# A graph network of two layers on one core: the numbers for VectorE's node one-hots are read from PSUM

## What is computed

```python
e = leaky_relu(xl[src] + xr[dst], 0.2)                 # layers 0 and 1
logits = einsum('ehc,hc->eh', e, att)
m = segment_max(logits, dst); ex = exp(logits - m[dst])
denom = segment_sum(ex, dst)
out = segment_sum(xl[src] * (ex / denom[dst])[..., None], dst) + b
# layer 2: e = leaky_relu(s1[:, src] + s2[:, dst]), Wh = h @ W in place of xl
```

## Time and profile before

| | |
|---|---|
| median of 3 runs | 4124.04 us |
| profiled execution | 4115.89 us, span 4114.1 us |
| granted TensorE clock, mean | 0.947 |
| PE, PEld busy | 3659.4 us (89%), 2722.7 us (66%) |
| DVE busy | 3149.5 us (77%) |
| POOL busy | 2804.3 us (68%) |
| ACT busy | 1229.2 us (30%) |
| POOL's 2496 gathers L692 | 2610.5 us busy, 800.1 us idle before them |
| edge stages of layers 0, 1, 2, by the first and last gather | 188 to 1311, 1549 to 2674, 2866 to 3993 us |

### The profile page before, as it was taken

The page is one execution under the profiler, slowest core; times in us unless marked ns, Lnnn a source line. Parts: engine busy times, 40 slices in busy tenths (PEclk is TensorE's granted clock), DMA queues, the critical chain, the costliest instruction groups (busy, mean ns, idle before and its releaser), DMA issues. The chain is left out here.

```text
span 4114.1 us, 121899 instructions
## 1 busy us (share of the span) xinstructions
PE 3659.4 (89%) x31817; PEld 2722.7 (66%) x31818; DVE 3149.5 (77%) x8748; ACT 1229.2 (30%) x4200; POOL 2804.3 (68%) x2941
## 2 busy tenths in 40 slices
PE   6699999999999898999999999977788777877875
PEld 5577777777776676777777777745455554555543
DVE  6667877787788665787787787875688788888886
ACT  4433333333333563333333333324111111111113
POOL 5577777777775127777777777723777777777760
PEclk9899999999999999999999999999788889888889
DMA  4354444444443225444444444435545545554544
GB/s 101 107 141 127 132 131 133 127 132 132 132 127 96 62 67 135 131 132 132 127 132 132 131 126 132 126 107 176 136 136 139 137 132 139 139 135 133 139 107 125
DMA packets 333899, 521.05 MB, mean 127 GB/s; under 512 B 152887, under 2 KB 219617, under 8 KB 333809
## 3 DMA queue, kind: packets, MB, share of 16 engines
q0 software_dynamic: 120320, 338.39, 30.1%
q1 hardware_dynamic: 213489, 181.58, 15.4%
HBM read 484.14 MB, written 35.46 MB: 126 GB/s over the span
## 5 line engine op out<-in xcount | busy, mean ns | idle before, releaser
L692 POOL DMA_INDIRECT gathered<-table,idx x2496 | 2610.5, 1046 | 800.1 <-issue 545.9
L1131 PE MATMUL pS<-gathered,Dm 128*128 128x264 f32 x4992 | 1706.2, 425 | 90.6 <-DVE Dm L1537 49.4
L1525 DVE TENSOR_TENSOR acc_mem<-acc_mem,pS 128x264 f32 x2496 | 1041.4, 417 | 133.0 <-PE pS L1131 108.7
L1068 PE MATMUL pZ<-DT,x 128*128 128x128 bf16 x9984 | 1083.7, 221 | 11.8 <-DVE DT L1488 9.0
L1068 PEld LDWEIGHTS pZ<-DT,x 128*128 x9984 | 867.9, 99 | 339.4 <-issue 61.6
L853 ACT ACTIVATE reluT<-pZ 128x256 f32<-128x256 f32 x1664 | 636.9, 383 | 1301.8 <-PE pZ L1074 1182.5
L1074 PE MATMUL pZ<-ident,gathered 128*128 128x128 f32 x3328 | 937.5, 282 | 15.9 <-DMA gathered<-table,idx 15.7
L1131 PEld LDWEIGHTS pS<-gathered,Dm 128*128 128x128 f32 x4992 | 793.0, 200 | 234.1 <-DVE gathered L1554 112.6
L1554 DVE TENSOR_TENSOR gathered<-gathered 128x512 f32<-128x512 f32 x1248 | 852.4, 683 | 65.0 <-ACT gathered L870 64.1
L1537 DVE TENSOR_TENSOR Dm<-iota_row,rel_items 128x256 f32<-128x256 f32 x1248 | 516.5, 414 | 0.0
L1074 PEld LDWEIGHTS pZ<-ident,gathered 128*128 128x128 f32 x3328 | 470.7, 141 | 20.3 <-DMA gathered<-table,idx 18.9
(11 more groups left out here) (230 smaller groups left out, 3372.3 us busy)
## 6 DMA issues: line engine op xcount, KB each, us to landing
DT<-rel_dram SPq DMA_DIRECT2D x156, 512.0 KB
gathered<-table,idx POOLq DMA_INDIRECT x2496
flags<-flag_dram SPq DMA_DIRECT2D x1664, 8.0 KB
span_row<-flag_dram SPq DMA_DIRECT2D x1664, 0.1 KB
table<-xls SPq DMA_DIRECT2D x147, 132.0 KB, 1.9
flags<-flag_dram SPq DMA_DIRECT2D x416, 32.0 KB
gathered<-table SPq DMA_DIRECT2D x98, 132.0 KB, 2.1
gathered<-in_x SPq DMA_DIRECT2D x98, 128.0 KB, 2.1
```

Source lines behind the costliest of these rows:

```text
L692: nc.gpsimd.indirect_dma_start(out=G[:, b, i, :], out_offset=None, in_=tab[l], in_offset=bass.IndirectOffsetOnAxis(ap=idx[:, b, i:i + 1], ...
L1068: mm = nc.tensor.matmul(z_slot(i)[:, half], x3[:, bass.ds(tk[i], 1), s, half].rearrange("p o c -> p (o c)"), moving, start=(s == 0), stop= ...
L1131: nc.tensor.matmul(pS[:, i % 4, 0:ROW], Dm[:, i % 8, :], G[:, at[0], at[1], :], start=True, stop=True).then_inc(seg_done, 1)
L1525: link(v.tensor_tensor(acc_at(n), acc_at(n), pS[:, n % 4, 0:ROW], ALU.add))
```

## The change

The numbers 0 to 127 are copied once, before the first group of layer 0, into columns 288 to 415 of each of the four banks of `pS`. From then on a one-hot that follows an `add` reads its numbers there, in the bank whose sums have just been added, and no longer from `iota_row` in SBUF. One-hots without an add before them (in the first groups of a layer) still use `iota_row`. `rel` stays in SBUF and stays the second operand.

```diff
                 if l == 0:
                     clear_sums()
+                    dve.wait_ge(xr_ready, TILES)
+                    dve.wait_ge(xls_ready, TILES)
+                    pre(v.tensor_copy(pS[:, :, IOTA:IOTA + P], iota_row[:].unsqueeze(1).to_broadcast([P, 4, P])))
...
                             rel = rel_items[:, bass.ds(k0 + (2 * s + 2 - 3 * GI // 2), 2)]
-                            ins = v.tensor_tensor(Dm[:, 2 * p % 8:2 * p % 8 + 2, :], iota_row[:].unsqueeze(1).to_broadcast([P, 2, P]),
+                            numbers = pS[:, 2 * s % 4, IOTA:IOTA + P] if adds else iota_row[:]
+                            ins = v.tensor_tensor(Dm[:, 2 * p % 8:2 * p % 8 + 2, :], numbers.unsqueeze(1).to_broadcast([P, 2, P]),
                                                   rel.unsqueeze(2).to_broadcast([P, 2, P]), ALU.is_equal)
                             if adds:
                                 ins.then_inc(added, 1)
...
 EARLY = 4
+IOTA = 288
```

## The result

| | before | after |
|---|---|---|
| median of 19 runs each, us | 4125.71 (4120.17 to 4129.43) | 4119.15 (4106.96 to 4123.68) |
| ratio, 95% interval | | 0.9983 (0.9976 to 0.9990) |
| profiled execution (span) | 4115.89 (4114.1) | 4120.86 (4119.0) |
| first to last gather, layers 0, 1, 2 | 1122.7, 1125.4, 1127.6 | 1122.7, 1122.4, 1129.7 |

The change is worth 6.6 us by the medians, 0.17%, where 19 were forecast. The two profiled executions alone stand the other way round: that of the kernel before, 4115.89, is shorter than all 19 runs beside it.

The account below looks back on a forecast made before the run. It took layer 2 to be bound by POOL's 832 gathers and layers 0 and 1 by PE's pace. Terms -18 - 1 + 0 = -19 us, from 4124.04, gave 4105; own range 4096 to 4117, overall range 4085 to 4127.

Parts of the forecast that it names:

- The price of the one-hot: DVE's one-hots reading PSUM: 414 ns as before, so no cost; bounds 10 ns less or more, 12 us of DVE.
- Something of DVE's holds a gather, and PSUM as one input ends it: All layers: two-SBUF DVE instructions stall POOL's gathers at their start; under one-hots 20.3, 20.1 and 15.7 us, ended by PSUM.
- Nothing is freed: Rival, chance 0.18: the one-hot's second input, still in SBUF, keeps all 408 gather stalls; 4124 us, within 5.
- The copies: Start of kernel: one tensor_copy of 512 elements on DVE, covered by a 13.99 us wait; costs nothing, 0.7 us without cover.
- Layers 0 and 1: Gain for both layers together from one-hots no longer holding gathers: 1 us, bounds 0 and 6.
- PE's own pace sets the end: Layers 0 and 1: PE, at 21.62 us per 16 items, and not POOL sets when the layer ends.
- the gain is given back at once: Layers 0 and 1: a gather freed of 0.14 us lets the next start earlier under the same L1554, ending no sooner.
- All of it comes off: Rival, chance 0.10: layers 0 and 1 are bound by POOL too, so all 56 us go; 4068 us.
- 18, with 8 as the low bound: Layer 2, bound by POOL's gathers: 18 us shorter without one-hot stalls, low bound 8 (half given back), high 25.
- the re-timing: Layer 2: unheld gathers start the next ones earlier; a gather-by-gather walk made the 15.7 us gain 18 to 22.
- within 0.2%: Whole kernel: outcome "same", a difference of at most about 8.2 us; chance 0.24, against faster 0.66 and slower 0.10.
- slower: Rival, chance 0.10: in layers 0 and 1 freed gathers are caught by L1554 instead, 0.53 us more per group; 4161 us.

Follow-up runs that it names:

- h6_swap: The changed kernel with the one-hots' two inputs exchanged, rel in SBUF first and the numbers in PSUM second; 4118.39 us against 4122.88, ratio 0.9986.
- q4_sbuf_weigh_l2: As p3_weigh_l2, but all one-hots read their numbers from SBUF again; 4065.76 us against 4124.64 for the kernel before, ratio 0.9861.
- q5_weigh_l01: The changed kernel with the weighting factors of layers 0 and 1 read from PSUM, softmax weighting left out there; 4112.57 us against 4124.64, ratio 0.9970.
- p3_weigh_l2: The changed kernel with layer 2's weighting factors read from PSUM, softmax weighting left out there; 4057.51 us against 4121.77 for the kernel before, ratio 0.984.
- e3_weigh_l2: Same kernel as p3_weigh_l2, run when the kernel before itself took 5244 to 5323 us; ratio 0.9995 (0.9969 to 1.0020).

## Why the prediction was right or wrong

**The price of the one-hot: right.** 414 ns forecast, 414 measured, with 1239 of them reading PSUM; in h6_swap they take 400 to 422. By the figures of the Trainium skill, "VectorE: DVE Perf Modes", section on the TRN2 errata, it would be some 65 ns dearer, an estimate; this case's rows don't show that: L1541 has one PSUM operand and the same 414 as the earlier trace rows with none.

**Something of DVE's holds a gather, and PSUM as one input ends it: right.** The 408 stalls under one-hots, 56 us over the three layers, are gone, in either order of the operands. *Nothing is freed* is out. One thing the prediction read too narrowly: not all 408 gathers began under their one-hot. In the kernel before 19 of them, 16 in layer 2, began up to 0.07 us ahead of it, and lost 6.5 us together:

```profile
2937.29 1.29 POOL L692 DMA_INDIRECT gathered<-table,idx  x1 [0.30 <-issue]
...
2937.35 0.41 DVE L1537 TENSOR_TENSOR Dm<-iota_row,rel_items 128x256 f32<-128x256 f32 x1
```

The Trainium skill, "SBUF — State Buffer", section "Who interferes with whom", says that two SBUF inputs contend with GpSimd instructions that read SBUF and one doesn't; the tensor_tensor rows of this case agree, with 0.95 us against 1.09 and 1.31 for a gather. Its other remark, that tensor_tensor left DMAs alone in a probe, doesn't hold for the gathers here: 1.09 against 0.95 us, in the rows of q4_sbuf_weigh_l2 and h6_swap.

**The copies: right.** DVE waits for 13.65 us behind them. DVE's timeline in the changed kernel, which answers to the earlier trace rows:

```profile
201.84 0.69 DVE L1496 COPY pS<-iota_row 128x512 f32<-128x512 f32 x1
...
217.02 0.43 DVE L1571 TENSOR_TENSOR_SCAN F<-flags,cT 128x128 f32<-128x128 f32 x1 [13.65 <-ACT cT L849]
```

**Layers 0 and 1: right in time, wrong in mechanism.** The forecast was 1 us, bounds 0 and 6; by the profiled executions layer 0 has 0.0 and layer 1 3.0 (in h6_swap -0.9 and 4.1). "PE's own pace sets the end" stood the test of q5. But "the gain is given back at once", under the next L1554, was wrong. What was named as its sign, L692's mean within 3 us of now and more stall under L1554, failed: the means fell from 1045 to 1005 and 1003 ns, and the stall under the weighting fell too, from about 50 us to 37.7 and 36.0. POOL now runs ahead until it meets the limit of the 32 slots, and waits there. Timeline of layer 0:

```profile
726.86 0.94 POOL L692 DMA_INDIRECT gathered<-table,idx  x1 [1.17 <-POOLq L358]
```

Such waits of over 0.02 us beyond the usual 0.30 number 41 in layer 0 and 44 in layer 1, where there had been 0 and 6. Most of these gathers begin 0.81 us after the L1068 that frees a slot. The waits hold 33.7 us in layer 0, which is what the gathers lost in length. The mistake was to follow POOL with DVE's times as they were in the earlier trace rows and with no limit on how far POOL may be ahead. A walk that keeps one side fixed can't show where the other comes to rest. *All of it comes off* is out with it.

**Layer 2: the step that failed.** "18, with 8 as the low bound" was put on layer 2's stretch; the gain came out at -2.1 in the changed kernel, and at 3.1 and 2.5 in h6_swap and q5_weigh_l01, whose layer 2 does the same (all against the one trace of the kernel before). The mean gather of the layer, which was to fall by 20 to 25 ns, went from 1048 to 1052. Who bounds the layer was right (p3_weigh_l2), that the 15.7 us leave the one-hots was right, and they are worth some time where no weighting can take them over (q4 against p3). The term that was mis-sized is the re-timing. It was worked out as a gain of 2 to 6 us on top of 15.7 ("18 to 22"), and was a loss of 12.6 to 17.8: 15.7 less the 3.1, 2.5 or -2.1 that arrived. The weighting took the stalls over: 64.4 us under it where there were 53.9. The re-timing rests on one assumption, "DVE's instructions stay at their distance from the landing that opens their group". I ran the same walk, with no stalls under one-hots, on the changed kernel's own distances: it gives 1127.2, where the trace has 1129.7, and on those of h6_swap 1122.3 against 1124.5. On the distances of before it gave 1107 to 1110. The rule of the stall is right, then, and the distances are what moved.

One way in which they move can be read. DVE's softmax part doesn't wait for the landing alone. Its scan L1572, now L1576, waits for ACT's L860, which waits for the transposes L1109, and PE does those in their place among the items that it works on just then. Over the 52 groups L1109 begins 2.7 to 5.0 us after L832 before and 3.0 to 5.0 after the change; its lower quartile moves from 3.50 to 4.55, and that of the scan behind it from 4.65 to 5.41, while the upper quartiles stay. The waits before the scan grow from 61.6 to 76.5 us in 51 groups, 0.3 us each, by the rows of L1572 and L1576 above. Of the 51 periods from one L832 to the next, 22 were below 21 us before and 27 over 22.0, up to 23.2; afterwards 7 are below 21 and 18 over 22.0, with two over 22.5. The mean is nearly the same, 21.75 and 21.79. The short periods, in which POOL slipped between the weightings, became rare (10 of 51 in h6_swap and in q5_weigh_l01), and 210 gathers are now caught by one where 176 were. That the groups settle into such a pattern is seen; that PE's order is what moved them is argued and not tested; and why it is this pattern, and whether another small edit would tip it the other way, is not settled.

**The time.** 4119.15 was inside the range of 4085 to 4127 but not inside the forecast's own, 4096 to 4117, and a gain of 0.17% falls into "within 0.2%", to which 0.24 was given. (The bounds of the prediction's terms add up to 4093 to 4116, so its own range is a little off its sum; that changes nothing here. The 0.41 us per group under *slower* is 0.39 by its own 2.8 x 0.14.) That the range of 4085 to 4127 held is no merit of the mechanism: it was made wide enough for *nothing is freed*. Of the 6.6 us, 2 to 4 can be placed: layer 1 takes 1121.3 to 1122.7 us in the three profiled executions with all one-hots from PSUM and both weightings of layers 0 and 1 as they were, and 1124.4 and 1125.4 in the two without. Layer 2 may add up to 3. The rest is not located: one profiled execution per kernel doesn't resolve it, what lies outside the edge stages alone differs by up to 11 us between the six of them, and the runs that did one part alone fell where the change shows no gain. *Slower* didn't come. Its mechanism did, gathers caught by weightings in place of one-hots, but in layer 2, where it ate the gain and no more.

## What to carry to other kernels

A stall that goes from a chain of back-to-back DMAs is worth its time only if no other instruction holds the gathers that come early now: take away the largest holder first (here the weighting, 54 to 64 us in layer 2). Then the small one was worth about two thirds of what it showed, 8 of 12.3 us, in the one pair of kernels that tried it. When gains are followed by a walk through the trace, let both sides move, and put in the limit of the buffers; if the answer hangs on distances that were only copied from the old trace, the low bound is nothing, not half. "No idle time" on an engine doesn't make it the bound: POOL had none in layers 0 and 1, and 72 us of stall less in each gave 4 and 5 us.

## What the runs showed of the hardware

- A DVE tensor_tensor with both inputs in SBUF that is under way when an indirect DMA of POOL begins holds it by the instruction's end less the DMA's start less 0.12 us. With either input in PSUM it doesn't: 0.95 us in all four pairs with PSUM above, 1.09 and 1.31 in those without.
- A one-hot from SBUF can hold a gather that began just ahead of it: 19 in the kernel before, all begun less than 0.07 us ahead, were held by 0.29 to 0.36 us (one more, 0.05 us ahead, was not). None that began more than 0.07 us ahead was, and a weighting that begins 0.08 us after a gather does nothing.
- An L1488 (one bf16 SBUF input) that follows a weighting from PSUM holds a gather that begins up to 0.47 us ahead of it, until it begins itself, less 0.07 to 0.08 us: 21 gathers of p3_weigh_l2, 25 of q4_sbuf_weigh_l2 and 85 of q5_weigh_l01, where these make up 12.6 of the 23.5 us of stall left in layers 0 and 1. L1488's own 0.75 us doesn't count then.
- The same kernel took 5244 to 5323 us at other times, with mean granted clocks of 0.876 to 0.892 instead of 0.945 to 0.955. The clock alone doesn't explain 1557 us for layer 0 in place of 1123: the stretch of it shown above has a granted clock of 0.92 against 1.00, and PE is idle for a fifth of it. There ACT's L853 begins more than 0.5 us after the modelled end of its L1074 for 393 of the 832 items (e3_weigh_l2), against 51 in the kernel before. What lies behind that was not tried.
